# One kept half per graph copied by VectorE instead of ScalarE in the statistics pass of a two-layer graph network

## The reference, cut to what matters

```python
D = jnp.abs(x[:, :, None, :] - x[:, None, :, :])
h = jnp.einsum('bijc,oc->bijo', D, W1) + b1
m = jnp.mean(h, axis=(0, 1, 2))
v = jnp.mean((h - m) ** 2, axis=(0, 1, 2))
h = (h - m) / jnp.sqrt(v + EPS) * g1 + be1
h = _leaky(h)
s = jnp.einsum('bijo,uo->biju', h, W2)[..., 0] + b2[0]
...
```

## Time and profile before

| | |
|---|---|
| median of three runs | 2622.51 us (2621.72 to 2623.73) |
| the profiled execution, its own time | 2612.55 us |
| its span in the trace | 2610.8 us |
| TensorE, VectorE, ScalarE busy | 80%, 81%, 87% of the span |
| statistics pass | from 386.53 us (first subtraction) to 1713.5 us |

### The profile page before, as it was taken

How to read it: one execution, slowest core, us unless ns; L and a number is a source line. 1 busy time by engine, 2 the same in 40 slices (tenths; PEclk the granted TensorE clock), 3 DMA queues, 4 the chain that set the end, 5 groups by cost and what they waited for, 6 DMA issues and landing times.

```text
span 2610.8 us, 36169 instructions
## 1 busy us (share of the span) xinstructions
PE 2076.8 (80%) x12997; PEld 857.9 (33%) x12997; DVE 2108.1 (81%) x2590; ACT 2261.2 (87%) x3505; POOL 32.9 (1%) x58
## 2 busy tenths in 40 slices
PE   5777757888888888888888888877787787787856
PEld 4555532232323323233233332312222232232226
DVE  4888857989999899998999999986777777776735
ACT  4999977999999999999999999968777877877845
POOL 0000000000000000000000000000000000000000
PEclk8999968999999999999999999988998988988868
DMA  3111123444444444444444444367777777877722
GB/s 108 44 38 44 38 70 136 168 171 174 164 173 175 171 174 163 180 168 171 174 163 176 173 170 174 154 269 279 279 275 280 272 281 279 285 284 273 282 95 65
DMA packets 230505, 470.52 MB, mean 180 GB/s; under 512 B 53496, under 2 KB 144312, under 8 KB 213944
## 3 DMA queue, kind: packets, MB, share of 16 engines
q1 hardware_dynamic: 229264, 467.84, 49.1%
q10 hardware_dynamic: 1064, 0.36, 0.1%
HBM read 254.19 MB, written 213.91 MB: 179 GB/s over the span
## 4 chain that ended last, share of the span: by engine, by line
PE 29%; ACT 24%; issue 16%; DVE 13%; DMA 10%; SPq 7%; POOL 1%; ACTq 0%; DVEq 0%; POOLq 0%
PE banks L899 13%; ACT banks L649 10%; DMA ring_scores<-sring 6%; DVE diff L1263 6%; ACT hcopy L646 5%; ACT habs L646 5%; DVE ring L1116 3%; PE banks L978 3%; DMA ub<-ring_scores 3%; PE banks L810 2%; SPq L441 2%; PE banks L1006 2%; ACT diff L634 2%; SPq L421 2%; DVE diff L1277 2%
## 5 line engine op out<-in xcount | busy, mean ns | idle before, releaser
L899 PE MATMUL banks<-diff,w1t 128*64 128x512 f32 x5136 | 1237.8, 613 | 192.8 <-ACT banks L649 142.1
L1263 DVE TENSOR_TENSOR diff<-ring 128x2048 f32<-128x2048 f32 x352 | 802.7, 2288 | 116.6 <-PE banks L899 116.6
L899 PEld LDWEIGHTS banks<-diff,w1t 128*64 128x64 f32 x5136 | 347.4, 139 | 945.1 <-issue 865.8
L649 ACT ACTIVATE banks<-banks,par 128x1024 f32<-128x1024 f32 x512 | 559.2, 1092 | 7.4 <-PE banks L899 4.8
L1277 DVE TENSOR_SCALAR diff<-diff 128x2048 int32<-128x2048 int32 x354 | 415.4, 1219 | 0.0
L1391 DVE TENSOR_TENSOR diff<-ring 128x2048 f32<-128x2048 f32 x128 | 292.7, 2287 | 67.6 <-PE banks L899 67.6
L670 ACT ACTIVATE habs<-banks,par 128x1024 f32<-128x1024 f32 x128 | 153.4, 1198 | 155.6 <-PE banks L899 155.6
L634 ACT ACTIVATE diff<-banks 128x2048 f32<-128x2048 f32 x128 | 240.4, 1878 | 12.6 <-PE banks L914 12.6
L646 ACT ACTIVATE hcopy<-banks 128x1024 f32<-128x1024 f32 x192 | 197.0, 1026 | 18.4 <-PE banks L899 18.1
L646 ACT ACTIVATE habs<-banks 128x1024 f32<-128x1024 f32 x192 | 196.9, 1026 | 18.4 <-PE banks L899 18.1
L914 PE MATMUL banks<-pick,yt 32*128 32x256 f32 x2560 | 185.0, 403 | 10.7 <-DMA yt<-xrows 10.7
(11 more groups left out here) (214 smaller groups left out, 2009.8 us busy)
## 6 DMA issues: line engine op xcount, KB each, us to landing
diff<-kept_two SPq DMA_DIRECT2D x86, 1024.0 KB, 6.3
kept_two<-hcopy SPq DMA_DIRECT2D x128, 512.0 KB, 2.6
kept_two<-habs SPq DMA_DIRECT2D x128, 512.0 KB, 2.6
hcopy<-kept_two SPq DMA_DIRECT2D x42, 1024.0 KB, 6.2
kept_one<-hcopy SPq DMA_DIRECT2D x64, 512.0 KB, 2.6
kept_one<-habs SPq DMA_DIRECT2D x64, 512.0 KB, 2.6
hcopy<-kept_one SPq DMA_DIRECT2D x64, 512.0 KB, 4.5
habs<-kept_one SPq DMA_DIRECT2D x64, 512.0 KB, 6.4
```

What stands on the lines that cost most here:

```text
L649: nc.scalar.activation(h, h, ACT.Square, bias=par[:, 53:54], accum_out=column(SQUARES + c)).then_inc(sq_done, 1)
L899: last = nc.tensor.matmul(dst[half * O:(half + 1) * O, bank * BANK:(bank + 1) * BANK], w1t[:, :], src[:, m * BANK:(m + 1) * BANK], start=T ...
L1263: v.tensor_tensor(shaped(diff[:, c % ND, :]), xj, xi_, ALU.subtract).then_inc(sub_done, 1)
```

## The change

`BY_DVE` is the position of chunk `(0, 1)` in `ORDER`, which is 12. Its copy out of PSUM into `tokeep` is now issued by VectorE (`keep_h`), as a plain copy without a sum. It stands in front of the subtraction of chunk 15 and waits for projection 12. ScalarE no longer copies chunk 12; its square of chunk 12 waits for VectorE's copy (`kept_by_dve`). The sum that the copy gave is had otherwise: the absolute values of chunk 12 are now written with `accum_out`, as those of the other TensorE-made chunks were (so L636 goes and one line does all five), and that sum goes into `EVENS`, which is later multiplied by W1. SyncE's store waits for the new semaphore. The columns of the sums are renumbered, 160 and 352 of them where there were 128 and 384.

```diff
+    BY_DVE = ORDER.index((0, 1))
...
-    EVENS, ODDS, SQUARES = 0, B * NR, B * NR + B * NK
+    EVENS, ODDS, SQUARES = 0, B * NP, B * NP + B * NK
...
-                sp.wait_ge(kept_copied, n + 1)
+                if j == BY_DVE:
+                    sp.wait_ge(kept_by_dve, b + 1)
+                else:
+                    sp.wait_ge(kept_copied, n + 1 - b - (j > BY_DVE))
...
-                if ORDER[j] in REDONE:
-                    nc.scalar.activation(dst, dps, ACT.Abs, accum_out=column(EVENS + b * NR + REDONE.index(ORDER[j]))).then_inc(abs_pe, 1)
-                else:
-                    nc.scalar.activation(dst, dps, ACT.Abs).then_inc(abs_pe, 1)
+                nc.scalar.activation(dst, dps, ACT.Abs, accum_out=column(EVENS + n)).then_inc(abs_pe, 1)
...
-                if ORDER[j] not in REDONE:
+                if j == BY_DVE:
+                    act.wait_ge(kept_by_dve, b + 1)
+                elif ORDER[j] not in REDONE:
...
+            def keep_h(b):
+
+                c, n = in_order(b, BY_DVE), b * NK + kept_before(BY_DVE)
+                dve.wait_ge(h_ready, c + 1)
+                if n >= KB:
+                    dve.wait_ge(kept_stored[n % KB], 16 * (n // KB))
+                v.tensor_copy(tokeep[n % KB], hps[c % 2]).then_inc(kept_by_dve, 1)
+
             def differences_between(b, lo, hi):
 
                 for j in range(lo, hi):
+                    if j == BY_DVE + 3:
+                        keep_h(b)
                     subtract(b, j)
...
-            v.tensor_reduce(col[20], yt[:, SUMS + EVENS:SUMS + EVENS + B * NR], AX.X, ALU.add)
-            v.tensor_reduce(col[48], yt[:, SUMS + ODDS:SUMS + ODDS + B * NK], AX.X, ALU.add)
+            v.tensor_reduce(col[20], yt[:, SUMS + EVENS:SUMS + EVENS + B * NP], AX.X, ALU.add)
+            v.tensor_reduce(col[48], yt[:, SUMS + ODDS:SUMS + ODDS + B * (NK - 1)], AX.X, ALU.add)
```

More of the change, by code:

```diff
@@ L231, in gnn_pair_kernel @@
         abs_dve = sem("abs_dve")
+        kept_by_dve = sem("kept_by_dve")
         sq_done = sem("sq_done")
@@ L645, in sum_h @@
                         act.wait_ge(kept_stored[n % KB], 16 * (n // KB))
-                    nc.scalar.activation(tokeep[n % KB], h, ACT.Identity, accum_out=column(ODDS + n)).then_inc(kept_copied, 1)
+                    nc.scalar.activation(tokeep[n % KB], h, ACT.Identity, accum_out=column(ODDS + n - b - (j > BY_DVE))).then_inc(kept_copied, 1)
                 if c == 0:
```

## The result

The changed kernel takes 2772.22 us (median of four runs, 2769.89 to 2776.53), the kernel before 2622.11 us (median of four, one run more than in the table above). The ratio is 1.0576, 95% interval 1.0557 to 1.0594: 5.8% slower. The forecast was 2779.5 us, in a range of 2718 to 2805. The two profiled executions are 2612.55 and 2769.89 us, 157.3 us apart, where the forecast's sum was 157.

A forecast was written before the change was run, and what follows sets the result against it. A ring of waits was taken to bound the kernel, with VectorE late once per graph before projection 13. Stall 3.26 plus clock 1.65 us, times 32 graphs, adds 157 to 2622.5: 2779.5 us, range 2718 to 2805.

The forecast's parts named there:

- The place: Around chunk 13, once per graph, TensorE and then ScalarE wait for VectorE's absolute values; the new copy stands before them.
- ScalarE's copy worth 0: Removing ScalarE's 1.03 us copy of chunk 12 only lengthens its 1.13 us wait for projection 13; worth 0.
- the sum worth 0: Adding a sum to VectorE's absolute values of chunk 12 costs 0, with 0.1 us as upper end.
- with VectorE never late the copy would be worth 1.0 us: At chunk 12 on ScalarE: if VectorE were never late, removing the copy would be worth about 1.0 us per graph.
- The stall: Before subtraction 15 on VectorE: 2.13 us idle for projection 12 plus 1.13 of copy delays each graph 3.26 us.
- The clock: TensorE's pause before projection 13 grows from 1.40 to 4.66 us; half clock behind it costs 1.65 us per graph.
- The sum of 4.91 us per graph: In the statistics pass: 3.26 us of stall plus 1.65 of slow clock per graph, times 32 graphs 157 us.
- Projections 14 and 15 have cover: On TensorE behind projection 13: slow clock there charged 0, as ScalarE turns to them later; 0.3 us as upper end.
- ScalarE's wait for projection 13: Sign in the changed kernel's trace: this wait, once per graph, becomes 6 us or so instead of 1.13.

The follow-up runs named there:

- e1: The changed kernel with VectorE's copy of chunk 12 moved behind the absolute values of chunk 13; 2623.89 us, ratio 1.0051 to the kernel before.
- e2: The kernel before with one added wait: VectorE waits for projection 12 in front of subtraction 15, no added work; 2719.98 us, ratio 1.0409.
- f1: The kernel before with VectorE's last batch reordered: subtractions 13, 14, absolute values of 13, subtraction 15, absolute values of 14, 15; 2573.63 us, ratio 0.9841.
- e4: The changed kernel with chunk 12 copied by neither engine and no wait for that copy, sum kept; 2611.57 us, ratio 0.9995 to the kernel before.
- f3: f2 with VectorE's copy between subtraction 15 and absolute values of 14, and ScalarE's square of chunk 12 in another buffer, ahead of the copy; 2578.36 us, ratio 0.9859.
- e3: The changed kernel with two needless projections on TensorE right behind projection 12, filling its pause; 2711.69 us, ratio 1.0387 to the kernel before.
- e6: e2 with one needless projection on TensorE behind projection 12, filling part of the pause; 2681.34 us, ratio 1.0260 to the kernel before.
- f4: f2 with one needless projection on TensorE in front of projection 0 of graphs 1 to 31; 2595.50 us, ratio 0.9924 to the kernel before.
- f2: The changed kernel with VectorE's last batch reordered: subtractions 13, 14, absolute values of 13, 14, copy of chunk 12, subtraction 15, absolute values of 15; 2623.86 us, ratio 1.0038.

## Why the prediction was right

**The place.** The step that carried the forecast was that VectorE's absolute values of chunk 13 are what TensorE and then ScalarE wait for, and that the copy stands in front of them. e1 (same work, another place: 1.0051) and e2 (the wait, no work: 1.0409) show it, and f1 from the other side: absolute values of 13 that come earlier take 1.24 us off each graph.

**ScalarE's copy worth 0, the sum worth 0.** e4 shows both, 0.9995. The high share of ScalarE in the busy line said nothing of this place. The prediction adds that with VectorE never late the copy would be worth 1.0 us. That was wrong for this kernel: in f3 VectorE is not late for projection 13, ScalarE neither copies chunk 12 nor waits for VectorE's copy, and the graph is as long as in f1, because projection 13 then waits for the square of chunk 11.

**The stall.** Worked out 3.26 us per graph; e3 measured 3.26, of which e6 measured 2.13 for the wait. The copy was put at 1.21 us and took 1.22.

**The clock.** The pause was put at 4.66 us and was 4.65. The clock's price, put at 1.65 us per graph, measured 1.60 (45.65 − 44.05); its mean in the pass was put at about 0.9 and was 0.94. The estimate leant on the second pass, where the rows show it low behind pauses of 3.65 and 4.93 us. Three rows there gave a loss between 1.4 and 1.74 us, and the choice of 1.65 within it was a judgement; single projections 13 lost 1.27 to 1.74 us. The price in the example of the Trainium skill, 0.83 us a round ("TensorE: Matmul & The Clock Gate", section "HAM oscillation — how this bites in real kernels"), comes from another kernel and is half of what is measured here; the measurement decides for 1.60. That the clock falls in each round, as the page has it, this trace agrees with: every projection 13 in the part of the timeline from 430 to 1840 us was slower than 1.94 us.

**What was off.** The sum of 4.91 us per graph stands against 4.86, 157 us against 156 in the pass. That it also meets the 157.3 us between two single executions is luck, as executions of one kernel lie several us apart (2769.89 to 2776.53). The 7 us between forecast and median come from adding the sum to the median of before, which stood 10 us above its profiled execution, while that of the changed kernel stands 2.3 us above its own. "Projections 14 and 15 have cover" held: the changed kernel is 1.60 us per graph slower than e3, and projection 13 alone takes 1.58 us longer (3.52 against 1.94).

ScalarE's wait for projection 13 was put at "6 us or so" and was 5.65, but the working has two slips that nearly cancel. Its terms (3.26, 1.65 and 1.0) are what is added to the old wait of 1.13, so their sum should have been 7.04 us. And the square of chunk 12 waits for VectorE's copy, 1.35 us per graph (40.4 / 30), which the prediction left out and which shortens the wait for projection 13. The two waits together are 7.00 us. Nothing in the forecast of the time hangs on it.

## What to carry to other kernels

In a ring of engines that wait for each other, look for the one place per round at which each of them is late, and price a new instruction by what is queued behind it there; the busy share of the engine that is relieved said nothing here (87%, and a copy taken from it was worth 0). Before an instruction is moved to a queue, read when its input is ready: an in-order queue loses the time until then, here twice what the instruction itself costs. And where a wait makes TensorE pause for 2 us or more (2.02 us was the shortest with a frequent fall of the clock here), look at the granted clock behind it, add the price, and try whether needless matmuls in the pause give it back: they were worth 1.9% in e3, 1.5% in e6 and 1.1% in f4.

## What the runs showed that I had not expected

**A pause of 2.02 us can be enough.** Before, the pause in front of projection 0 is 1.70 us and the clock stays at 1.00. In f2 it is 2.02 us, and projection 0 is slow in 18 of the 31 graphs between 430 and 1690 us; in e1 it is 1.98 to 1.99 us, and in the same stretch it was slow in 2 of 31. Which of them it strikes is not set by the pause alone: the pauses of f2 are all alike, and what came before them in the graph too. What else decides, the runs do not settle.

**The round settles against the clock.** In e2, projection 13 took 3.68 us in the first graphs, was once fast, and from 702 us on took 3.38 to 3.41 us in every graph, and the graph 44.37 us (from 1146.27 to 1190.64). In the changed kernel, where the pause is 4.65 us, it kept changing between 3.21 and 3.68 us, in a sequence that comes round every eight graphs: 3.46 us at 850.41, 1215.63 and 1580.86 us, and 3.68 us in the graph behind each. Why the one settles and the other does not was not tried.
